# Last stage inside the experts' program, expert loops written out, first table loads spread, two evictions deferred

## The chip, the cores and the metric

The kernel runs on one core of a Trainium2 chip. The metric is the device time of one execution in microseconds. A core has five engines that run their own instruction streams and meet at semaphores: TensorE (PE, matmul, with its weight load PEld), VectorE (DVE), ScalarE (ACT), GpSimd (POOL) and SyncE (SP, which here only issues DMAs). Sixteen DMA engines move data between HBM and SBUF; SyncE, ScalarE and GpSimd issue to them.

## The reference, cut to what matters

Input x is 4096 tokens of 512 values. Two residual layers follow each other:

```python
x = x + layernorm(scan(layernorm(x)))      # selective scan, 512 channels x 16 states
x = x + layernorm(moe(layernorm(x)))       # 8 experts, top 2, capacity 640 per choice, plus a shared expert

# scan: xp = x @ W_x ; dt = softplus(xp[:64] @ W_dt + b_dt)
#       h = exp(dt * A) * h + (dt * x) * B ; y = sum(h * C) + x * D_skip
# moe, for each of the two choices k and each expert e (tokens beyond the capacity are dropped):
h = gelu(einsum('ecd,edf->ecf', buf, w1) + b1)                 # 512 -> 2048
y = einsum('ecf,efd->ecd', h, w2) + b2                         # 2048 -> 512
y = y + einsum('ecr,erd->ecd', gelu(einsum('ecd,edr->ecr', buf, wd)), wu)   # rank 32
out = out + tok * w                                            # weighted, back to the token's row
# shared expert for all tokens, times 0.2
```

## The kernel before

The program is a row of blocks with a barrier between them.

**prepare** (lines 57 to 324) works on eight chunks of 512 tokens. Per chunk: load x, normalise, transpose, project to xp, form dt with softplus, form dt * x. Results go to HBM as xT_d, bc_d (the rows of B and C), dt_d and dtx_d. The tiles xpT, dt and dx have two buffers each, xn and xnT three. SyncE's stream is one loop over rounds i (line 139): load x of chunk i+2, store xT of i-1, bc of i-2, dt and dtx of i-3, each behind the wait for its tile. In round 5 it also calls load_first_scans (line 127): eight loads of Bt and eight of Ct, each two rows of bc_d broadcast to 128 partitions, 512 KB, and five loads of 256 KB for the first passes of the scan. They fill tiles that live on into the next block.

**mix** (line 375) runs the scan, unit by unit over 8 chunks of 64 units, and fills TensorE's gaps with the shared expert for seven of the eight groups of 512 tokens. The sum is in acc_d, x after the first layer in x1_d.

**experts** (line 1020) does the shared expert for the last group, the routing, and then eight experts. An expert has three blocks of 2, 4 and 4 token tiles (EB, line 1006). A block is `run`, one per engine: 17 steps j, of which step 0 is the low-rank pair and the other 16 the hidden chunks. In a step TensorE makes the up product (L1684) of step j+1 into psH, then the down product of step j (L1723 for the low rank, L1727 for the others) into psY; ScalarE applies gelu (L1283, L1289); VectorE splits the result into a high and a low half (L1489 to L1497), since every product is taken as three matmuls of halves. After the last step VectorE takes the n tiles of psY out with weight and bias (L1514) into yst, and GpSimd adds them to acc_d with an indirect DMA (L1405). TensorE's first low-rank matmul of the next block waits until all of those n are out (L1716).

Weights of the next expert are loaded by SyncE piece by piece into a ring of four raw buffers (L1183), cast to the high half by ScalarE (L1242) during block 2 as soon as TensorE is done with the old chunk, and subtracted to the low half by GpSimd (L1361). Each body starts on ScalarE with a copy of the expert's biases (b1e, L1339). GpSimd's order within a body is `steady` (L1450): gathers of token rows (L1366) and of slot weights (L1390), scatters (L1405), the subtractions for the next expert. Its gathers for the next expert need the slot indices, which VectorE writes (L1602) after block 1.

On each engine the experts 0 to 6 are a hardware loop (`Fori`, L1348, L1469, L1661, L1789) and the expert 7 is written out behind it; SyncE's loop (L1224) loads the weights of experts 1 to 7. A matmul of 512 columns follows the other at 0.23 us.

**tail** (line 1794) is a block of its own: for 16 groups of 256 tokens load the sum y (L1817) and x1 (L1818), statistics (L1844, L1847), square root on ScalarE (L1831), reciprocal and product (L1851, L1853), normalise on ScalarE (L1834), add x1 (L1860), store from GpSimd (L1824).

Of the kernel before, what the change touches and what calls it, by code (L numbers as in the profile page):

```python
# [56 lines left out]
def prepare(nc, sem, const, early, x, A_log, D_skip, W_x, W_dt, b_dt, dt_d, dtx_d, bc_d, xT_d):  # L57
# [4 lines left out]
    with ExitStack() as ctx:  # L62
# [41 lines left out]
        def _(sp):  # L104
# [34 lines left out]
            for i in steps(2, 4):  # L139
# [8 lines left out]
                if i == 5:  # L148
                    load_first_scans()
# [867 lines left out]
WEIGH_AT = (4, 6, 8, 10)  # L1017


def experts(nc, sem, const, w, ws_d, lgT_d, x1_d, xt_d, acc_d, w_d):  # L1020
# [8 lines left out]
    with ExitStack() as ctx:  # L1029
# [3 lines left out]
        W1h, W1l = sb("W1h", [P, FC, DT, P], F32R), sb("W1l", [P, FC, DT, P], F32R)  # L1033
        W2h, W2l = sb("W2h", [P, FC, D], F32R), sb("W2l", [P, FC, D], F32R)
# [37 lines left out]
        Xa = (sb("Xah", [P, DT, 512], F32R), sb("Xal", [P, DT, 512], F32R))  # L1072
        X = (Xa, Xb, (sb("Xch", [P, DT, 256], F32R), sb("Xcl", [P, DT, 256], F32R)))
# [16 lines left out]
        s_spare, s_slots, s_sidx = (sem(f"c_{n}") for n in ("spare_rows", "slot_rows", "scatter_rows"))  # L1090
# [14 lines left out]
        g_sp, g_pool, g_pe, g_act, g_dve = (sem(f"c_gate_{n}") for n in ("sp", "pool", "pe", "act", "dve"))  # L1105
        block = ctx.enter_context(nc.Block("experts"))

# [6 lines left out]
        def shared(b):  # L1114

            return dict(B=0, t0=0, th=0, n=BT, gathered=False, row=b * BT)
# [46 lines left out]
        def added(e, i):  # L1163

            return (1 + e * Y_USES[i]) * 16

# [6 lines left out]
        def _(sp):  # L1173
# [50 lines left out]
            with sp.Fori(1, E) as e:  # L1224
                load_pieces(e + 1, weights_of(e))
                bias2(e, expert(e, 0))
            for i in range(4):
                sp.wait_ge(s_yst[i], added(E, i))
            for q in range(2):
                sp.wait_ge(s_xts[q], BT // 2 * 16)  # L1230

        @block.scalar
        def _(act):
# [27 lines left out]
            def weigh_bias(at, t):  # L1261

                if at["gathered"]:
# [5 lines left out]
                    scale = wsl[:, EB[k][0] + t:EB[k][0] + t + 1]  # L1269
                else:  # L1270
                    i, scale = t, SHARE
                    act.wait_ge(s_b2, 16)
                nc.scalar.mul(yst[i][:, :], b2bc[:, :], scale).then_inc(s_b2w, 1)
# [74 lines left out]
            with act.Fori(0, E - 1) as e:  # L1348
                expert_blocks(e)
            expert_blocks(E - 1, last=True)  # L1350

        @block.gpsimd
        def _(pool):
# [21 lines left out]
            def store_shared(b):  # L1375
                for t in range(BT):
                    pool.wait_ge(s_yev, t + 1)
                    nc.gpsimd.dma_start(acc_d[(b * BT + t) * P:(b * BT + t + 1) * P, :], yst[t][:, :])\
                        .then_inc(s_yst[t], 16)
# [30 lines left out]

            nc.gpsimd.memzero(L1h[:, :, :]).then_inc(s_pad, 1)
# [30 lines left out]
            store_shared(SB - 1)  # L1442
# [4 lines left out]
            gathers(0, 1, range(4))  # L1447
# [21 lines left out]
            with pool.Fori(0, E - 1) as e:  # L1469
                steady(e)  # L1470
            steady(E - 1, last=True)

        @block.vector
        def _(dve):
# [6 lines left out]
            def run(at, logits=False, nxt=None, extra=None):  # L1481
                G, n = at["B"] * J, at["n"]
                for j in range(J):
# [10 lines left out]
                    else:  # L1494
# [3 lines left out]
                            .then_inc(s_hlo, 1)  # L1498
                    if logits and j == 0:
# [8 lines left out]
                dve.wait_ge(s_mm2, G + J)  # L1508
                for t in range(n):
                    dve.wait_ge(s_b2w, at["t0"] + t + 1)  # L1510
                    i, scale = t, SHARE
                    if at["gathered"]:
                        i, scale = Y_TILE[at["k"]][t], wsl[:, EB[at["k"]][0] + t:EB[at["k"]][0] + t + 1]
# [428 lines left out]
```

## Time and profile before

| | us |
|---|---|
| median of 3 runs | 3615.76 (3614.01 to 3616.12) |
| the profiled execution, its own time | 3623.88 |
| its span, first to last instruction | 3622.1 |
| busy in the span: TensorE, VectorE | 3161.7, 1848.0 |
| busy in the span: GpSimd, ScalarE | 1724.7, 1426.5 |
| DMA moved, mean | 463.61 MB, 128 GB/s |

The profile comes from one execution, the times from others; durations are read from the first and the result is set against the second. The stages follow each other almost without overlap, so they are read one at a time: for each, which engine is busy nearly all of it, and where even that one stands still. The chain that ended last, as the page gives it, reaches back only to the barrier at 3552 us and speaks of the last stage alone.

### The profile page before, as it was taken

The page shows a single profiled execution, that of the slowest core. Times are in us where ns is not written, and L with a number is a line of the kernel's source. Part 1 is how long each engine was busy: PE and PEld are TensorE (multiplying, and loading weights), DVE is VectorE, ACT ScalarE, POOL GpSimd, SP SyncE. Part 2 cuts the span into 40 slices and gives each one's busy share as a digit, 9 for nine tenths or more (in the row PEclk, how much of TensorE's full clock was granted, in tenths as well). Part 3 has the DMA queues.
Part 4 walks back from the last instruction along what each step waited for, and adds up shares of the span by engine and source line. Part 5 has one row for each costly group of instructions (what it writes and reads, how often), then busy time and mean ns, then how long its engine had stood idle before and what let it go on. Part 6 is the DMA issues. An engine that isn't in the chain of part 4 may idle for free. (4 is left out here: it accounts for less than half of the span.)

```text
span 3622.1 us, 45551 instructions
## 1 busy us (share of the span) xinstructions
PE 3161.7 (87%) x15191; PEld 2578.5 (71%) x15191; DVE 1848.0 (51%) x2708; ACT 1426.5 (39%) x2529; POOL 1724.7 (48%) x1576
## 2 busy tenths in 40 slices
PE   6445698988989988789999999999999999999990
PEld 3233477777777776678888888788888887888880
DVE  6489889898898981462222232223222322232225
ACT  7445576766766763311221321322213213222113
POOL 1067787888879884431341532513415325134101
PEclk8655699999999999879999999999999999999995
DMA  7848696796976945921330421412304214123008
GB/s 235 229 149 218 188 256 189 215 242 197 248 206 197 267 148 167 267 68 21 70 77 12 99 56 33 108 21 64 81 14 99 56 33 108 21 64 79 12 12 290
DMA packets 276932, 463.61 MB, mean 128 GB/s; under 512 B 32065, under 2 KB 107729, under 8 KB 276706
## 3 DMA queue, kind: packets, MB, share of 16 engines
q1 hardware_dynamic: 206656, 266.21, 26.1%
q0 software_dynamic: 68288, 194.06, 20.8%
q8 instruction: 133, 2.18, 0.2%
q14 instruction: 93, 0.76, 0.1%
q10 hardware_dynamic: 1762, 0.40, 0.1%
HBM read 363.44 MB, written 97.14 MB: 127 GB/s over the span
## 5 line engine op out<-in xcount | busy, mean ns | idle before, releaser
L1495 DVE CAST hh<-h 128x512 fp32r<-128x512 f32 (+1 forms) x400 | 170.6, 426 | 1290.2 <-ACT h L1289 1245.0
L823 POOL TENSOR_TENSOR u<-dtxs,Bt 128x512 f32<-128x512 f32 x512 | 671.1, 1348 | 168.9 <-DVE b_psA L726 151.0
L1289 ACT ACTIVATE h<-c_psH,b1e 128x512 f32<-128x512 f32 (+1 forms) x384 | 236.8, 617 | 1254.4 <-PE c_psH L1684 1212.5
L726 DVE TENSOR_TENSOR_SCAN b_psA<-b_psA,carry,u 128x512 f32<-128x512 f32 x512 | 656.3, 1282 | 65.0 <-ACT b_psA L596 62.4
L1727 PE MATMUL c_psY<-W2h,hh 128*128 128x512 f32 x1344 | 536.3, 399 | 4.9 <-DVE hl L1497 4.6
L931 PE MATMUL b_psY<-ident,pr 128*128 128x128 f32 x2048 | 350.2, 310 | 207.9 <-DVE pr L733 190.2
L1727 PE MATMUL c_psY<-W2l,hh 128*128 128x512 f32 x1344 | 526.9, 392 | 0.0
L1727 PE MATMUL c_psY<-W2h,hl 128*128 128x512 f32 x1344 | 526.4, 392 | 0.0
L1366 POOL DMA_INDIRECT xrow<-xt_d,idx x80 | 90.6, 1132 | 882.4 <-PE c_psT L1675 479.8
L931 PEld LDWEIGHTS b_psY<-ident,pr 128*128 128x128 f32 x2048 | 269.4, 158 | 293.4 <-DVE pr L733 240.5
L733 DVE TENSOR_TENSOR pr<-b_psA,Ct 128x512 f32<-128x512 f32 x512 | 354.0, 691 | 19.2 <-DMA Ct<-bc_d 1.6
L596 ACT ACTIVATE b_psA<-dts,A_neg 128x512 f32<-128x512 f32 x512 | 354.3, 692 | 16.1
L966 PE MATMUL b_psH<-Xh,w 128*128 128x512 f32 x896 | 319.5, 418 | 8.1 <-DMA w<-ws_d 8.0
L1361 POOL TENSOR_TENSOR W1l<-raw,W1h 128x512 fp32r<-128x512 f32 x128 | 193.4, 1511 | 263.5 <-ACT W1h L1242 263.3
L1727 PEld LDWEIGHTS c_psY<-W2h,hh 128*128 128x128 f32 x1344 | 254.1, 189 | 60.1 <-DVE hl L1497 12.0
L985 PE MATMUL b_psS<-w,hhs 128*128 128x512 f32 x896 | 294.4, 410 | 0.0
L1727 PEld LDWEIGHTS c_psY<-W2h,hl 128*128 128x128 f32 x1344 | 253.9, 189 | 55.1
L1727 PEld LDWEIGHTS c_psY<-W2l,hh 128*128 128x128 f32 x1344 | 254.3, 189 | 47.6 <-issue 0.2
L1497 DVE TENSOR_TENSOR hl<-h,hh 128x512 fp32r<-128x512 f32 (+1 forms) x400 | 257.6, 644 | 13.7
L1684 PE MATMUL c_psH<-Xbh,W1h 128*128 128x512 f32 x576 | 224.4, 390 | 0.0
L1684 PE MATMUL c_psH<-Xbh,W1l 128*128 128x512 f32 x576 | 224.2, 389 | 0.0
L1684 PE MATMUL c_psH<-Xbl,W1h 128*128 128x512 f32 x576 | 224.1, 389 | 0.0
(262 smaller groups left out, 5763.0 us busy)
## 6 DMA issues: line engine op xcount, KB each, us to landing
w<-ws_d POOLq DMA_DIRECT2D x224, 512.0 KB, 6.8
raw<-in_w SPq DMA_DIRECT2D x256, 256.0 KB
Bt<-bc_d SPq DMA_DIRECT2D x64, 512.0 KB, 16.9
Ct<-bc_d SPq DMA_DIRECT2D x64, 512.0 KB, 20.5
xn<-in_x SPq DMA_DIRECT2D x8, 1024.0 KB, 6.3
xT_d<-xnT SPq DMA_DIRECT2D x8, 1024.0 KB, 8.5
dt_d<-a_dt SPq DMA_DIRECT2D x8, 1024.0 KB, 9.5
dtx_d<-a_dx SPq DMA_DIRECT2D x8, 1024.0 KB, 10.0
```

The costliest lines, as they stand in the source:

```text
L596: nc.scalar.activation(psA[g % 2][:, :], dts[s % 2][:, :], ACT.Exp, scale=A_neg[:, s % DT, n:n + 1]).then_inc(s_dA, 1)
L726: nc.vector.tensor_tensor_scan(psA[q][:, :], psA[q][:, :], u[g % U_RING][:, :], carry[:, k:k + 1], ALU.mult, ALU.add).then_inc(s_h, 1)
L733: nc.vector.tensor_tensor(pr[g % PR_RING][:, :], psA[g % 2][:, :], C_of(g), ALU.mult)\
L823: nc.gpsimd.tensor_tensor(u[g % U_RING][:, :], dtx[s % 2][:, :], Bt[n // TG][:, n % TG, :], ALU.mult)\
L931: last = nc.tensor.matmul(psY[:, t, :], pr[g % PR_RING][:, t * P:(t + 1) * P], ident[:, :], start=(n == 0 and t == 0), stop=False, is_tran ...
L966: last = nc.tensor.matmul(psH[:, :], a[:, d, :], v[:, d, :], start=(d == 0 and i == 0), stop=(d == DT - 1 and i == 2))
L985: last = nc.tensor.matmul(psS[t][:, :], a, v, start=False, stop=(j == FC and i == 2))
L1289: nc.scalar.activation(h32[:, 0:n * P], psH[j % 2][:, 0:n * P], ACT.Gelu, bias=b1[:, j - 1:j]).then_inc(s_gelu, 1)
L1361: nc.gpsimd.tensor_tensor(lo, view, hi.bitcast(F32), ALU.subtract).then_inc(s_wlo, 1)
L1497: nc.vector.tensor_tensor(hl[j % 2][a], h32[a], hh[j % 2][a].bitcast(F32), ALU.subtract)\
L1684: last = nc.tensor.matmul(out, a, b, start=(i == 0), stop=(i == n - 1))
L1727: last = nc.tensor.matmul(psY[t][:, :], a[j % 2][:, c], b, start=False, stop=(j == J - 1 and i == 2))
```

## The change

1. SyncE in prepare: load_first_scans is split. A pair of table loads (Bt and Ct of index i-3) follows the stores of each round from 3 to 10, and the loads of the first passes are made in round 9.
2. The four engines' loops over experts 0 to 6 and SyncE's over 1 to 7 become Python loops, so that eight bodies stand in a row.
3. In `run` on VectorE the last step takes out psY tiles 0 and 1 only. Tiles 2 and 3 of a block of four are taken out in the next block, after its step 0 (`late`). TensorE's low-rank matmuls of a gathered block wait for the eviction of their own tile. The shared block uses the same tiles and weight column as an expert's block 2, with the factor 0.2 set in the column at the start, and GpSimd stores it behind two gathers for expert 0.
4. The block `tail` is gone. Its instructions stand behind the experts on each engine, without a barrier. The x1 loads (L1818 before) are made during the last block of the last expert, paced by the up products; the loads of y when the last scatter has landed. Sixteen tiles each of y and x1 lie where x, W1 and W2 lay. SyncE waits for the final stores.

```diff
-            def load_first_scans():
+            def load_first_tables(j):
                 sp.wait_ge(s_obc[0], 16)
-                for j in range(NG):
-                    load_table(sp, bc_d, early["Bt"], early["s_B"], 0, j, 0)
-                    load_table(sp, bc_d, early["Ct"], early["s_C"], NS, j, 0)
+                load_table(sp, bc_d, early["Bt"], early["s_B"], 0, j, 0)
+                load_table(sp, bc_d, early["Ct"], early["s_C"], NS, j, 0)
+
+            def load_first_passes():
...
-                if i == 5:
-                    load_first_scans()
+                if 0 <= i - 3 < NG:
+                    load_first_tables(i - 3)
+                if i == NCH + 1:
+                    load_first_passes()
...
-            with sp.Fori(1, E) as e:
+            for e in range(1, E):
                 load_pieces(e + 1, weights_of(e))
                 bias2(e, expert(e, 0))
+            for g in range(NT // TAIL_G):
+                G = expert(E - 1, 2)["B"] * J
+                sp.wait_ge(s_mm1, G if g < 5 else G + min(J, 2 * g - 7))
+                sp.dma_start(x1r[g][:, :, :], tail_rows(x1_d, g)).then_inc(d_x1[g], 16)
+            sp.wait_ge(s_mm2, E * 3 * J + J)
             for i in range(4):
                 sp.wait_ge(s_yst[i], added(E, i))
+            for g in range(NT // TAIL_G):
+                sp.dma_start(y[g][:, :, :], tail_rows(acc_d, g)).then_inc(d_y[g], 16)
...
+            def leave(at, t):
+                dve.wait_ge(s_mm2, (at["B"] + 1) * J)
+                dve.wait_ge(s_b2w, at["t0"] + t + 1)
+                out, scale = y_out(at, t)
+                nc.vector.scalar_tensor_tensor(out, psY[t][:, :], scale, out, ALU.mult, ALU.add).then_inc(s_yev, 1)
...
+                    if late is not None and j == 0:
+                        for t in (2, 3):
+                            leave(late, t)
...
-                for t in range(n):
...
+                for t in range(2):
+                    leave(at, t)
...
-                run(expert(e, 0), nxt=(expert(e, 1), X_OF[1]), extra={12: (lambda: scatter_rows(e),)})
+                run(expert(e, 0), late=expert(e - 1, 2), nxt=(expert(e, 1), X_OF[1]), extra={12: (lambda: scatter_rows(e),)})
...
-                run(expert(e, 2), nxt=None if last else (expert(e + 1, 0), X_OF[0]))
-
-            with dve.Fori(0, E - 1) as e:
+                run(expert(e, 2), late=expert(e, 1), nxt=None if last else (expert(e + 1, 0), X_OF[0]))
+
+            for e in range(E - 1):
                 expert_blocks(e)
...
-                        after(pe, s_yev, at["t0"])
...
+                            if at["gathered"]:
+                                pe.wait_ge(s_yev, at["t0"] - (2 if at["k"] == 1 else 4) + min(t, 1 if at["k"] == 1 else 3) + 1)
```

## Rows read from the trace of the kernel before

**Rows 1.** Busy time by stage: stretch, length, each engine busy (instructions), clock, DMA share, GB/s.

```profile
0.00:198.00 198.00, 96.60 (x256) 47.99 (x256) 107.70 (x112) 110.31 (x113) 14.08 (x40) 0.72 0.75 223
198.00:1441.00 1243.00, 1038.83 (x5216) 841.26 (x5216) 1065.16 (x1219) 772.93 (x1459) 994.08 (x943) 0.88 0.74 208
1609.00:3536.00 1927.00, 1894.60 (x9132) 1579.44 (x9130) 539.34 (x1011) 467.59 (x827) 625.64 (x484) 0.99 0.24 54
3552.00:3622.10 70.10, 0.00 (x0) 0.00 (x0) 46.54 (x128) 28.68 (x49) 11.76 (x16) 0.50 0.94 359
```

**Rows 2.** The same view, three stretches inside the first stage (PE, PEld, DVE, ACT, POOL).

```profile
40.00:60.00 20.00, 14.95 (x36) 7.12 (x35) 14.87 (x15) 15.44 (x17) 1.66 (x4) 0.70 0.65 226
...
100.00:118.00 18.00, 12.95 (x33) 6.45 (x32) 10.40 (x5) 13.49 (x15) 0.24 (x2) 0.72 0.95 166
118.00:145.00 27.00, 0.20 (x2) 0.00 (x0) 3.52 (x2) 1.03 (x1) 0.00 (x0) 0.54 0.98 222
```

**Rows 3.** Timelines of ACT, then DVE: start, us, instruction, [idle before, releaser].

```profile
145.46 0.58 ACT L215 COPY xpT<-a_psX 96x512 f32<-96x512 f32 x1 [26.43 <-DMA bc_d<-xpT]
...
75.05 2.29 DVE L259 TENSOR_TENSOR a_dx<-a_dt,xnT 128x2048 f32<-128x2048 f32 x1
...
109.21 2.29 DVE L259 TENSOR_TENSOR a_dx<-a_dt,xnT 128x2048 f32<-128x2048 f32 x1
...
153.94 2.29 DVE L259 TENSOR_TENSOR a_dx<-a_dt,xnT 128x2048 f32<-128x2048 f32 x1
...
189.28 2.29 DVE L259 TENSOR_TENSOR a_dx<-a_dt,xnT 128x2048 f32<-128x2048 f32 x1
```

**Rows 4.** Timeline of SyncE's queue: first and last of sixteen table loads, next store.

```profile
77.77 1.05 SPq L330 DMA_DIRECT2D Bt<-bc_d  x1
...
113.13 3.19 SPq L330 DMA_DIRECT2D Ct<-bc_d  x1
...
127.20 5.57 SPq L119 DMA_DIRECT2D bc_d<-xpT  x1
```

**Rows 5.** TensorE by body, cut at each seam's last matmul: busy, clock, DMA share, GB/s.

```profile
3055.83:3298.60 242.77, 237.82 (x1144) 0.99 0.26 59
3298.60:3536.20 237.60, 235.36 (x1136) 0.99 0.13 23
sum 1688.71, PE 1657.86; mean PE 236.84
```

**Rows 6.** Second and seventh seam on PE, and ScalarE's wait (total, times, longest).

```profile
2090.62 0.36 PE L1684 MATMUL c_psH<-Xch,L1h 128*104 128x256 f32 x1 [0.76 <-POOL W1l L1361]
...
2097.06 1.22 PE L1723 MATMUL c_psY<-L,hh 96*128 96x512 f32 x2 [3.38 <-DVE hh L1492]
...
3303.94 0.70 PE L1723 MATMUL c_psY<-L,hh 96*128 96x512 f32 x2 [2.19 <-DVE hh L1492]
...
ACT b1e L1339 <- issue: 14.7, 6, 2.5
```

**Rows 7.** PE's waits over the experts: total us, times, longest.

```profile
PE c_psY L1727 <- DVE hl L1497: 4.4, 5, 1.3
```

**Rows 8.** Busy time right after the second seam (columns as in rows 1).

```profile
2096.00:2104.00 8.00, 6.94 (x26) 6.17 (x27) 2.77 (x7) 0.95 (x2) 6.78 (x5) 0.57 0.89 145
```

**Rows 9.** Timeline of DVE: the evictions of the shared block.

```profile
1570.02 2.48 DVE L1514 SCALAR_TENSOR_TENSOR yst<-c_psY,yst 128x512 f32<-128x512 f32 x4 [3.49 <-PE c_psY L1727]
```

**Rows 10.** From block 1 to block 2 of one expert, on DVE and PE.

```profile
2244.19 0.68 DVE L1492 TENSOR_TENSOR hh<-h,hl 32x512 fp32r<-32x512 f32 x1
...
2245.21 1.09 PE L1723 MATMUL c_psY<-L,hh 96*128 96x512 f32 x4
```

**Rows 11.** From the last scatter's landing to the load, then DVE's first and last statistics.

```profile
3549.20:3552.03 2.83, 0.00 (x0) 0.00 (x0) 0.00 (x0) 0.00 (x1) 0.00 (x0) 0.50 0.00 0
...
3555.86 1.29 DVE L1844 BATCH_NORM_STATS2 d_st<-d_y 128x6 f32<-128x512 f32 x2 [16.90 <-DMA d_y<-acc_d]
...
3609.94 1.28 DVE L1844 BATCH_NORM_STATS2 d_st<-d_y 128x6 f32<-128x512 f32 x2 [0.93 <-DMA d_y<-acc_d]
```

More of the change, by code:

```diff
@@ L1346, in expert_blocks @@
                     run(expert(e, 2), b1e, nxt=nxt(e + 1, 0), wset=e + 2)
-            with act.Fori(0, E - 1) as e:
+            for e in range(E - 1):
                 expert_blocks(e)
             expert_blocks(E - 1, last=True)
+            for g in range(NT // TAIL_G):
+                act.wait_ge(d_mv, (g + 1) * TAIL_G)
+                nc.scalar.activation(ours(sd, g), ours(mv, g)[:, :, 1], ACT.Sqrt, bias=eps[:, :]).then_inc(d_sd, 1)
+                act.wait_ge(d_nm, g + 1)
+                for t in range(TAIL_G):
+                    k = g * TAIL_G + t
+                    nc.scalar.activation(y[g][:, t, :], y[g][:, t, :], ACT.Identity, bias=nm[:, k:k + 1],
+                                         scale=rs[:, k:k + 1]).then_inc(d_n, 1)
         @block.gpsimd
@@ L1446, in _ @@
             gather_weights(0, 0)
-            gathers(0, 1, range(4))
+            gathers(0, 1, range(2))
+            store_shared(SB - 1)
+            gathers(0, 1, range(2, 4))
             gather_weights(0, 1)
@@ L1467, in steady @@
                     gather_weights(e + 1, 1)
-            with pool.Fori(0, E - 1) as e:
+            for e in range(E - 1):
                 steady(e)
             steady(E - 1, last=True)
+            for g in range(NT // TAIL_G):
+                pool.wait_ge(d_x, (g + 1) * TAIL_G)
+                nc.gpsimd.dma_start(tail_rows(out_d, g), y[g][:, :, :]).then_inc(d_out, 16)
         @block.vector
@@ L1658, in expert_blocks, with stats, scale, residual @@
                     expert_slots(e + 1)
-                run(expert(e, 2), nxt=None if last else (expert(e + 1, 0), X_OF[0]))
-            with dve.Fori(0, E - 1) as e:
+                run(expert(e, 2), late=expert(e, 1), nxt=None if last else (expert(e + 1, 0), X_OF[0]))
+            for e in range(E - 1):
                 expert_blocks(e)
             expert_blocks(E - 1, last=True)
+            for t in (2, 3):
+                leave(expert(E - 1, 2), t)
+            def stats(g):
+                dve.wait_ge(d_y[g], 16)
+                for t in range(TAIL_G):
+                    v.bn_stats(st[:, g * TAIL_G + t, :], y[g][:, t, :]).then_inc(d_st, 1)
+                for t in range(TAIL_G):
+                    dve.wait_ge(d_st, g * TAIL_G + t + 1)
+                    v.bn_aggr(mv[:, g * TAIL_G + t, :], st[:, g * TAIL_G + t, :]).then_inc(d_mv, 1)
+            def scale(g):
+                dve.wait_ge(d_sd, g + 1)
+                v.reciprocal(ours(rs, g), ours(sd, g)).then_inc(d_rs, 1)
+                dve.wait_ge(d_rs, g + 1)
+                v.scalar_tensor_tensor(ours(nm, g), ours(mv, g)[:, :, 0], -1.0, ours(rs, g), ALU.mult, ALU.mult)\
+                    .then_inc(d_nm, 1)
+            def residual(g):
+                dve.wait_ge(d_x1[g], 16)
+                for t in range(TAIL_G):
+                    dve.wait_ge(d_n, g * TAIL_G + t + 1)
+                    v.tensor_tensor(y[g][:, t, :], y[g][:, t, :], x1r[g][:, t, :], ALU.add).then_inc(d_x, 1)
+            for g in range(NT // TAIL_G + 2):
+                if g < NT // TAIL_G:
+                    stats(g)
+                if 1 <= g <= NT // TAIL_G:
+                    scale(g - 1)
+                if g >= 2:
+                    residual(g - 2)
         @block.tensor
@@ L1923, in program @@
         const["wgt"] = ctx.enter_context(nc.sbuf_tensor("wgt", [P, K, NT], F32))
[L1924 to L1925 removed]
+        experts(nc, sem, const, a, ws_d, lgT_d, x1_d, xt_d, acc_d, w_d, out)
 def kernel(**inputs):
```

124 lines of the change are left out of this document (36 added, 88 removed).

## The prediction

> **What bounds the kernel now.** I read the busy time by stage first, then what idles inside each stage, since no engine sets the end everywhere. [rows 1]: in the first stage (normalise, project, step sizes, 0 to 198 us) no engine is above 0.56 busy, but the DMA engines stand at 0.75. In the scan stage (198 to 1441) VectorE is busy 1065 of 1243 us. In the experts (1609 to 3536) TensorE is busy 1895 of 1927 us. In the last stage (3552 to the end) TensorE does nothing, VectorE is busy 46.5 of 70.1 us, and 359 GB/s move. The diff touches the first, third and last of these; the scan stage keeps its code and can only be moved as a block.
>
> The second view is where the first stage idles. [rows 2]: from 118 to 145 us TensorE works 0.2, VectorE 3.5 and ScalarE 1.0 us, while the DMA engines are at 0.98. [rows 3]: ScalarE waits 26.43 us there for one small store (bc_d) to land, so that the fourth and fifth L259 on VectorE stand 44.7 us apart, where two earlier gaps took 17.1 us each. [rows 4]: SyncE issued sixteen table loads (Bt, Ct) in one run from 77.77 to 116.3 us; the stores of the next chunk could only be issued behind them.
>
> The third view is the time per expert [rows 5], the fourth the seam between two experts [rows 6].
>
> **Part 1, table loads spread over the first stage.** Removed: the run of sixteen loads before the stores of chunk 3. Added: a pair after the stores of each of the eight chunks, and the five loads of the first passes two rounds before the end. Same bytes, same queue. The stall is 44.7 - 17.1 = 27.6 us. What is late next: a DMA queue without room. A chunk takes 17.1 us, in which the queue without tables is busy at 0.65 [rows 2], 11.1 us. During the run the tables move at 166 GB/s and 0.95 [rows 2], so a pair of 2 x 0.524 MB costs 6.3 x 0.95 = 6.0 us. Sum 17.1 us of 17.1: just full for three rounds, and looser after them, as no more x is loaded. A dt buffer is wanted again only two rounds after its store is due, so a lag of a few microseconds is covered; without that cover each microsecond of lag is one of the end. The last pair is queued behind the last stores and is first used some 34 us into the scan stage (unit 14, at 1243/512 = 2.4 us a unit). I take **-26 us**, between -10 (a full queue gives most back) and -28.
>
> Other edges of SyncE's queue: the waits of a round are unchanged, and the load of x for the next round now stands behind a pair of tables; it has a round and more to land.
>
> The Trainium skill, DMA: Bandwidth & Descriptors, in "Issuing engines are not separate DMA queues", says that all DMAs run on the same 16 engines and interleave, whoever starts them. By that rule moving loads creates no room, and only the idle 0.35 of the earlier rounds can be won. Rows 2 fit it, 0.65 and 0.95 being the two levels; by the rule alone the sum would still be up to -26, so it prices the first rival and changes nothing else.
>
> **Part 2, the bodies written out.** The row for the cost of a loop is the wait of ScalarE for nothing that the profile shows, ahead of the first copy of an expert: 14.7 us in six times, 2.5 us each [rows 6]. There are seven seams, and the seventh is the one from the loop to the body that is already written out. TensorE's first matmul after a seam waits 0.76 us where the loop jumps, and the low-rank matmul (L1723) 3.38 us, against 2.19 us at the seventh [rows 6]; from the last matmul of one expert (2089.47, 3298.60, the cuts of rows 5) to that one (2097.06, 3303.94) it is 7.6 us there and 5.3 us at the seventh. So the seventh seam shows what all will be: what remains is ScalarE's last weight casts and the chain gelu, three casts on VectorE.
>
> A better measure is the whole body. Six bodies take 1688.71 - 237.60 = 1451.1 us, 241.9 each; the last takes 237.60 [rows 5]. The last ends with its last matmul's end and not its start (0.4), and lacks the eight transposes for a next expert (1144 against 1136 matmuls; at the mean of 0.21 us per matmul they cost at most 1.7, being short I take 1.0). So a written-out body costs 237.6 - 0.4 + 1.0 = 238.2, which is 3.6 less, 6 x 3.6 = 21.9 us. That counts two things too much. The last body converts no weights, and a wait in midblock is absent from it: TensorE waits for VectorE's low half 4.4 us in five times [rows 7], when GpSimd's scatters stand ahead of the subtractions of weights. GpSimd starts that batch some 1.3 us earlier after the change, since the slot indices (L1602) follow two evictions and not four; I keep a third, 1.5 us.
>
> The clock: for 8 us after the seam the granted clock is 0.57 in a body that jumps [rows 8], which is mostly the lower level of 1.2 GHz, after the wait of 3.38 us. The last body has such a dip too (0.99 over it), so it is in the 238.2. If the shorter waits leave no dip, each full one is worth up to 8 x 0.43/0.5 = 6.9 us at half speed, 3.4 us; that is the far end of the gain.
>
> The Trainium skill, Runtime: NRT & Kernel Launch, "Instruction fetch mechanics", says that instructions are streamed ahead strictly in order and that a taken jump to code outside the window stalls its engine. The six waits of 2.5 us and their absence at the seventh seam agree.
>
> **Part 3, two of four evictions late.** VectorE now takes tiles 0 and 1 out of PSUM at once and tiles 2 and 3 after the low-rank casts of the next block, and TensorE waits per tile. For the shared block this frees VectorE two evictions earlier (2.48 us for four, so 1.2 us) [rows 9] on the chain into the slot search: **-1.2 us**, from 0 to -1.3. Within an expert it adds a wait: from block 1 to block 2 the cast chain ends at 2244.87 and TensorE starts the four low-rank matmuls at 2245.21, done in 1.09 us [rows 10]. The two late evictions (0.62 us each by rows 9, a little more from a full block) end near 2246.2, so the fourth matmul, due at 2245.9, waits some 0.3 to 0.4 us: 8 x 0.4 = 3.2 us lost. Behind it on TensorE's queue stands the next up product; the gelu that feeds VectorE waits on that. At the seams the next block has two tiles and meets no such wait. From 0 (the matmul still fits) to 10 us (each wait also holds VectorE's next cast). The store of the shared block's last two tiles moves behind two gathers on GpSimd, and bias products on ScalarE wait for it four steps later; covered.
>
> Parts 2 and 3 in the experts: -21.9 + 1.5 + 3.2 = **-17 us**, between -6 and -28.
>
> **Part 4, the last stage in the same program.** The x1 loads (8.4 MB) move under the last expert, whose DMA share is 0.13 [rows 5]: hidden, as 8.4 MB over its last block (0.4 of 237.6 us) are 88 GB/s; uncovered they would cost 8.4 MB at 359 GB/s, 23 us. The barrier goes: from the landing of the last scatter at 3549.20 to 3552.03 nothing moves [rows 11], -2.8. First data then takes 3.83 us as now. The last group's statistics start at 3609.94, 54.1 us after the first, 3.61 per group [rows 11], set by 25.2 MB at 359 GB/s. With 16.8 MB that would take 47 us to the last store, with 3.8 to the first data and the closing 12.2 us (3609.94 to the end) partly inside it, so VectorE takes over: 46.54 / 16 = 2.91 per group, 15 x 2.91 = 43.6. Gain 10.4 + 2.8 = **-13.2 us**. Ends: -9 (GpSimd's closing drain with sixteen stores behind it) and -15.
>
> **Sum.** -26 - 1.2 - 17 - 13.2 = -57.4 us. The profiled execution took 3623.88 us (span 3622.1, 1.8 outside it), 8.1 above the median of the shown runs; nothing in the terms scales with that, so I take the sum off the median: 3615.76 - 57.4 = **3558 us**.
>
> **Rivals.**
> (a) The queue is full: the pairs do not fit, the stores lag, and only 10 us come from part 1: 3558 + 16 = 3574. For it: 17.1 of 17.1. Against it: three rounds only, and slack of a round per buffer.
> (b) The loops give little: the late evictions and ScalarE's casts eat the seams, -6: 3558 + 11 = 3569. For it: the seventh seam still waits 2.19 us. Against it: the last body's 237.6.
> (c) The clock stays at its upper level over the shorter seams: 3.4 x 3 or more off: about 3548.
> (d) Slower: the written-out bodies cannot be fed. Eight bodies of code are then read in one go by every engine, and if an engine waits for code inside a body, TensorE waits with it. It decides once the price passes 57.4 / 7 = 8.2 us per body, over three waits of the 2.5 us that a jump costs now; at five it gives 3558 + 7 x 12.5 = 3646. Against it: the scan stage is written out already, and VectorE is busy 0.86 of it [rows 1].
> (e) It does not do what it says: the first-stage stall has another cause and the seams stay; -13 of part 4 only, 3603.
>
> **Chances.** Forecast (3549 to 3568) 0.62; (a) 0.12, (b) 0.11, (c) 0.09, (d) 0.03, (e) 0.03. The range reaches (a), (b) and (c) with their own spread: 3542 to 3581. A measurement of this kernel tells about 0.2%, 7 us, from no change. Faster 0.96, same 0.01, slower 0.03.
>
> **What would show it.** Part 1: L259 eight times at 17 to 18 us, the scan stage beginning near 172. Part 2: ScalarE's wait before L1339 gone, bodies of 238 to 239 us. Part 3: an idle of 0.3 to 0.5 us before one L1723 in each block 2. Part 4: loads of y right at the last landing, VectorE never idle in the end stage, some 57 to 59 us from landing to end. The largest risk is part 1: half of the sum rests on a queue that is full to its edge.

## The result, and the profile after

| | before | after |
|---|---|---|
| median of four executions (us) | 3615.48 | 3586.01 |
| lowest to highest (us) | 3614.01 to 3616.12 | 3580.53 to 3587.25 |
| profiled execution (us) | 3623.88 | 3580.53 |
| its span (us) | 3622.1 | 3578.8 |

The ratio is 0.9914, with a 95% interval of 0.9898 to 0.9930: **29.5 us less**, where 57 us less were forecast. The time lies above the range, which ended at 3581. The profiled execution of before lay 8 us above its median and that of after 5 us below its own, so the two traces differ by 43.3 us; of these, 14 belong to the two executions and not to the kernels.

Busy time by stage of the kernel after (columns as in rows 1, which these lines answer; the stages start earlier, so the cuts differ):

```profile
0.00:167.00 167.00, 94.74 (x256) 47.38 (x256) 107.71 (x112) 110.21 (x113) 14.09 (x40) 0.80 0.84 257
167.00:1411.00 1244.00, 1035.57 (x5216) 838.95 (x5216) 1065.61 (x1220) 775.14 (x1461) 996.13 (x959) 0.88 0.74 209
1580.34:3507.66 1927.32, 1910.80 (x9128) 1577.98 (x9128) 543.81 (x1011) 466.18 (x826) 632.64 (x487) 1.00 0.25 59
3507.66:3578.80 71.14, 0.03 (x1) 0.00 (x0) 48.38 (x132) 27.39 (x48) 17.97 (x20) 0.52 0.76 259
```

The first stage is some 31 us shorter at the same busy times. The experts' stage, from the first up product of the first expert to the last matmul, takes 1927.3 us where [rows 1] have 1927.0: no gain, but the inside has changed. TensorE is busy 1910.8 us of it and not 1894.6. **The waits went, and the same matmuls (some 9130) got longer.** That is the finding of this study.

The traces, stretch by stretch (each length from the first matmul of one part to the first of the next):

| stretch (us) | before | after | change | forecast |
|---|---|---|---|---|
| start to shared block | 1473.5 | 1441.5 | -31.9 | -26 |
| shared block | 137.6 | 138.8 | +1.2 | -1.2 |
| experts, first up product to last matmul | 1924.7 | 1926.9 | +2.2 | -17 |
| last matmul to end | 86.3 | 71.5 | -14.8 | -13.2 |

**First stage.** VectorE's timeline, the eight L262 (L259 before), answers [rows 3]; first three, fifth to last:

```profile
40.76 2.29 DVE L262 TENSOR_TENSOR a_dx<-a_dt,xnT 128x2048 f32<-128x2048 f32 x1
57.93 2.29 DVE L262 TENSOR_TENSOR a_dx<-a_dt,xnT 128x2048 f32<-128x2048 f32 x1
75.05 2.29 DVE L262 TENSOR_TENSOR a_dx<-a_dt,xnT 128x2048 f32<-128x2048 f32 x1
...
109.22 2.29 DVE L262 TENSOR_TENSOR a_dx<-a_dt,xnT 128x2048 f32<-128x2048 f32 x1
126.29 2.29 DVE L262 TENSOR_TENSOR a_dx<-a_dt,xnT 128x2048 f32<-128x2048 f32 x1
143.36 2.29 DVE L262 TENSOR_TENSOR a_dx<-a_dt,xnT 128x2048 f32<-128x2048 f32 x1
160.20 2.29 DVE L262 TENSOR_TENSOR a_dx<-a_dt,xnT 128x2048 f32<-128x2048 f32 x1
```

They stand 17.1 us apart from the first to the last; the gap of 44.7 us is gone. The stretches that answer [rows 2] show where the tables now move:

```profile
40.00:60.00 20.00, 14.95 (x36) 7.07 (x35) 15.95 (x15) 15.72 (x17) 1.66 (x4) 0.76 0.98 274
...
100.00:118.00 18.00, 12.05 (x33) 6.04 (x32) 10.44 (x6) 14.62 (x16) 0.00 (x0) 0.81 0.83 267
118.00:145.00 27.00, 15.00 (x29) 6.92 (x30) 20.09 (x10) 14.45 (x13) 0.00 (x0) 0.75 0.76 210
```

From 40 to 60 us the DMA engines go from 0.65 to 0.98, full as the sum had it, and no engine loses time by it.

**Waits in the experts.** The waits of TensorE over the experts, all that the view gives, answer [rows 6, 7] (engine, line waited at, releaser: total, times, longest; L1809 is the low-rank matmul, L1723 before):

```profile
PE c_psY L1809 <- DVE hh L1549: 8.5, 4, 2.6
PE c_psY L1809 <- issue: 6.4, 3, 2.5
PE c_psH L1769 <- DVE Xcl L1529: 1.5, 1, 1.5
PE c_psY L1809 <- DVE yst L1536: 1.3, 8, 0.2
```

The seven seams wait 8.5 + 6.4 us in all, 2.1 each, as the seventh of before did. The wait for hl in midblock is gone, and so is ScalarE's wait ahead of the first copy. New is the wait for the late evictions in each of eight experts; on the timeline of TensorE and VectorE in one of them:

```profile
1731.42 1.41 DVE L1536 SCALAR_TENSOR_TENSOR yst<-c_psY,slot_weights,yst 128x512 f32<-128x512 f32 x2
...
1731.71 1.01 PE L1809 MATMUL c_psY<-L,hh 96*128 96x512 f32 x3
1732.88 0.50 PE L1809 MATMUL c_psY<-L,hh 96*128 96x512 f32 x1 [0.16 <-DVE yst L1536]
```

The fourth low-rank matmul starts 0.66 us after the third, where 0.23 is usual (all four of before follow each other at 0.23 to 0.24). The third comes 0.28 us after the second and the next up product 0.34 us after the fourth, so that the late evictions cost 0.59 us here; the view counts only the 0.16 us in which nothing at all ran.

**Tail.** SyncE's load, then VectorE's first and last statistics (these answer [rows 11]):

```profile
3520.41 17.84 SPq L1264 DMA_DIRECT2D d_y<-acc_d  x16
3524.28 1.29 DVE L1724 BATCH_NORM_STATS2 d_st<-d_y 128x6 f32<-128x512 f32 x2 [13.82 <-DMA d_y<-acc_d]
...
3565.12 1.28 DVE L1724 BATCH_NORM_STATS2 d_st<-d_y 128x6 f32<-128x512 f32 x2
```

From the landing of the last scatter to the end it is 58.4 us. VectorE's sixteen groups stand 2.72 us apart on the mean instead of 3.61: the first two last only 1.42 and 1.63 us, as no x1 is added yet, and from the fourth on it is 2.87 us. From 3524.28 to 3567.30 VectorE is busy 42.14 us of 43.02.

**Where the gain of the experts went.** The groups of TensorE's matmuls by form, over 1620 to 3450 us, of the kernel before (count, then total busy us and mean ns of one):

```profile
L1727 PE MATMUL c_psY<-W2l,hh 128*128 128x512 f32 x1214 | 476.3, 392 | 0.0
...
L1684 PE MATMUL c_psH<-Xah,W1l 128*128 128x512 f32 x512 | 201.8, 394 | 0.0
L1684 PE MATMUL c_psH<-Xah,W1h 128*128 128x512 f32 x512 | 201.8, 394 | 0.0
...
L1684 PE MATMUL c_psH<-Xbh,W1h 128*128 128x512 f32 x451 | 175.7, 389 | 0.0
```

and of the kernel after:

```profile
L1813 PE MATMUL c_psY<-W2l,hh 128*128 128x512 f32 x1214 | 480.6, 396 | 0.0
L1813 PE MATMUL c_psY<-W2h,hl 128*128 128x512 f32 x1214 | 480.2, 396 | 0.0
L1769 PE MATMUL c_psH<-Xah,W1l 128*128 128x512 f32 x512 | 200.6, 392 | 0.0
...
L1769 PE MATMUL c_psH<-Xbh,W1h 128*128 128x512 f32 x474 | 187.4, 395 | 0.0
```

Already before, the same product on the same shape took 394 ns from Xa and 389 from Xb. After, Xb and the down products are at 395 and 396. The ends are modelled, so the better measure is the spacing of starts between matmuls of one kind (mean of all under 0.3 us): before 0.2269 us for Xb, 0.2333 for Xa and 0.2281 for the down products; after 0.2319, 0.2293 and 0.2335. What the diff changed for them is only the order in which the tiles are declared, and with it their addresses: W1 and W2 stood ahead of all other tiles of the experts and now stand behind Xa and Xc (the lines that do it, others left out):

```diff
-        W1h, W1l = sb("W1h", [P, FC, DT, P], F32R), sb("W1l", [P, FC, DT, P], F32R)
-        W2h, W2l = sb("W2h", [P, FC, D], F32R), sb("W2l", [P, FC, D], F32R)
...
         rt.close()
...
+        X = (Xa, Xb, (sb("Xch", [P, DT, 256], F32R, loop), sb("Xcl", [P, DT, 256], F32R, loop)))
+        W1h, W1l = (sb(f"W1{h}", [P, FC, DT, P], F32R, loop) for h in "hl")
+        W2h, W2l = (sb(f"W2{h}", [P, FC, D], F32R, loop) for h in "hl")
```

### The profile page after: what moved, and what is told of

It reads as the page before. It is cut to its first block, busy times and chain, and to the rows that moved or that the text cites. A ratio compares the mean times of both kernels' runs of the same rounds, so it can differ in the third digit from the quotient of the medians.

```text
span 3578.8 us, 43069 instructions
## 1 busy us (share of the span) xinstructions
PE 3174.4 (89%) x15191; PEld 2574.6 (72%) x15191; DVE 1854.1 (52%) x2708; ACT 1425.5 (40%) x2529; POOL 1732.0 (48%) x1577
## 4 chain that ended last, share of the span: by engine, by line
PE 55%; DVE 2%; DMA 1%; issue 1%; POOL 1%; ACT 1%; SPq 0%; POOLq 0%; DVEq 0%; ACTq 0%
PE c_psH L1769 27%; PE c_psY L1813 26%; PE c_psT L1760 1%; PE c_psT L1864 1%; DVE d_y L1740 1%; DVE d_st L1724 1%; PE c_psY L1809 0%; DVE yst L1536 0%; DMA xrow<-x_d 0%; DMA raw<-in_w 0%; POOL W1l L1406 0%; DVE hh L1546 0%; ACT h L1320 0%; POOL W2l L1406 0%; DMA acc_d<-yst,sidx 0%
## 5 line engine op out<-in xcount | busy, mean ns | idle before, releaser
L599 ACT ACTIVATE b_psA<-dts,A_neg 128x512 f32<-128x512 f32 x512 | 354.3, 692 | 16.1
L1451 POOL DMA_INDIRECT acc_d<-yst,sidx x80 | 130.4, 1629 | 203.3 <-DVE yst L1536 182.3
```

The lines of the kernel that those rows point to most:

```text
L599: nc.scalar.activation(psA[g % 2][:, :], dts[s % 2][:, :], ACT.Exp, scale=A_neg[:, s % DT, n:n + 1]).then_inc(s_dA, 1)
```

## The experiments

The tables give start addresses in SBUF modulo 256 bytes, counted from the sizes in the order of declaration. A **pad** is an unused tile that does nothing but move what is declared behind it. Of a matmul's two operands the stationary one is what PEld loads (W1 in an up product, a slice of hh or hl in a down product), and the moving one is X or W2. Theory P: the place of the two operands against each other sets the spacing. Its rivals: the written-out code is fed more slowly (P's pad would then change nothing), or another engine's traffic on SBUF slows the reads.

**The pad in the kernel after.** W1, W2, Xa and Xc move by 64 bytes:

```
         loop = ExitStack()
+        sb("pad", [P, 16], F32, loop)
         Xa = (sb("Xah", ...
```

> The changed kernel with 64 unused bytes per partition ahead of the tiles Xa, Xc, W1 and W2, which moves these to start at 32 modulo 128 bytes, as Xb, hh and hl do. Nothing else differs. Theory P (placement): a matmul of 512 columns follows the other at 0.227 us where its moving and its stationary operand start at the same place modulo 128, and at 0.232 to 0.234 us where they don't; in the changed kernel that slows every down product and the up products of block 2. Then the last block of four tiles takes 90.6 + 0.6 us instead of 93.3, a body about 4.4 us less, and the whole kernel 30 to 36 us less than the changed kernel: ratio to before 0.982 to 0.984, about 3553 us. Rival D (distance): what counts is how far apart the operands lie, which 64 bytes don't change; then it equals the changed kernel, ratio 0.991. Rival S (the stream of written-out code slows TensorE's issue): also no change.

Measured: 3555.54 us (3554.92 to 3558.40), ratio 0.9824 [0.9811, 0.9838]. Block 1, block 2 and the last block of the last expert, first of the kernel after, then of the padded one (here only PE, clock, DMA share and GB/s in the first fence; all engines in the second):

```profile
1631.88:1726.10 94.22, 94.22 (x417) 1.00 0.07 12
1726.10:1820.56 94.46, 94.30 (x409) 1.00 0.40 103
...
3413.95:3507.66 93.71, 93.55 (x401) 1.00 0.29 80
```

```profile
1634.86:1727.58 92.72, 92.72 (x418) 76.43 (x417) 23.27 (x41) 15.95 (x25) 10.62 (x8) 1.00 0.07 12
1727.58:1819.99 92.41, 92.25 (x410) 75.58 (x409) 28.28 (x42) 31.76 (x57) 54.59 (x41) 1.00 0.42 105
...
3393.05:3484.64 91.59, 91.44 (x402) 74.66 (x400) 22.16 (x39) 15.34 (x22) 6.54 (x4) 1.00 0.30 81
```

TensorE is busy without a gap in block 1 in both, with the same matmuls at the same clock, and takes 1.50 us less with the pad; in block 2 it is 2.05 us less. The experts take 1900.5 us instead of 1926.9. Nothing but addresses differs: placement sets the spacing, and the code feed is ruled out as its cause. Which tiles' places count is the question of the next runs.

**The pad in the kernel before**, ahead of Xa alone:

```
+        sb("pad", [P, 16])
         Xa = (sb("Xah", ...
```

> The kernel before with 64 unused bytes per partition ahead of Xa and Xc, so that these too start at 32 modulo 128 bytes like W1. Theory P: block 1 of each expert (up products with Xa, 192 matmuls) and block 0 (Xc) get faster, 192 x 6 ns = 1.2 us and some 0.2 us per body, 10 to 12 us in all: ratio 0.997, block 1 at 93.0 instead of 94.2 us. Rivals D and S: no change, ratio 1.000.

Measured: 3613.40 us, ratio 0.9980 [0.9970, 0.9989] of the kernel before. Block 1 takes 92.72 us instead of 94.2, in eight bodies 11.6 us less; the experts 1916.6 instead of 1924.7, since the waits in midblock were longer in this execution (block 2 in seven bodies 657.4 us against 654.0). The group of Xa's products is now equal to Xb's:

```profile
L1685 PE MATMUL c_psH<-Xah,W1h 128*128 128x512 f32 x512 | 199.4, 389 | 0.0
...
L1685 PE MATMUL c_psH<-Xbh,W1h 128*128 128x512 f32 x456 | 177.6, 389 | 0.0
```

**What distance counts.** Three more places in the kernel before, by pads of 128 and 32 bytes behind W1 and W2, and of 64 bytes ahead of them (block 1 and time in us):

> The kernel before with 128 bytes of unused SBUF behind the expert weights, so that all activations move by 128 bytes against W1 and W2 and keep their place modulo 128. If the place modulo 128 bytes decides: matmuls keep their spacings, 0.2268 us for the up products from Xb and all down products and 0.2335 for those from Xa, block 1 at 94.2 us, and the time stays at the kernel before's, about 3617. If it is modulo 256 or more: the products that were at 0.2268 go to 0.2335, 480 x 0.0067 = 3.2 us more per expert, 26 us in all, about 3643.

> The kernel before with 64 bytes of unused SBUF ahead of everything of the experts, so that weights and activations move together. Modulo 256 bytes, W1, W2, Xb and hh then stand at 224 (160 before) and Xa at 160 (96 before): every distance is as before. Theory D (the distance between the two operands decides): spacings stay at 0.2269 for the up products from Xb and 0.2333 for those from Xa, time near 3618. Rival A (the place itself decides, 160 being a good one): the products from Xb and the down products lose up to 0.0064 us each, block 1 goes from 94.2 to near 95 us, and the time is up to 26 us longer, 3640.

> The kernel before with 32 bytes of unused SBUF behind the expert weights: modulo 256 W1 and W2 at 160, Xb and hh at 192, Xa at 128. Theory D (only equal places are fast): products from Xb and the down products, now 32 bytes apart, go from 0.2269 to about 0.233, Xa's (now 32 apart the other way) stay slow; time near 3643, as with 128 bytes (3639). Rival H (places within the same 64 bytes are as good as equal): Xa's products at 128 stand in the 64 bytes of W1's 160 and get fast, Xb's and the down products at 192 get slow; 480 down and 176 up products slower, 176 faster, by 0.0064 us in eight bodies: about 24 us longer.

| kernel | W1, W2 | Xb, hh | Xa | spacing Xb | spacing Xa | down | block 1 | time |
|---|---|---|---|---|---|---|---|---|
| before | 160 | 160 | 96 | 0.2269 | 0.2333 | 0.2281 | 94.2 | 3615.5 |
| before, all + 64 | 224 | 224 | 160 | 0.2270 | 0.2333 | 0.2283 | 94.2 | 3615.8 |
| before, pad at Xa | 160 | 160 | 160 | 0.2270 | 0.2270 | 0.2281 | 92.7 | 3613.4 |
| before, + 128 | 160 | 32 | 224 | 0.2331 | 0.2302 | 0.2331 | 94.4 | 3639.4 |
| before, + 32 | 160 | 192 | 128 | 0.2333 | 0.2334 | 0.2329 | 94.9 | 3656.4 |
| after | 96 | 160 | 96 | 0.2319 | 0.2293 | 0.2335 | 94.2 | 3586.0 |
| after, pad at Xa | 160 | 160 | 160 | 0.2270 | 0.2270 | 0.2280 | 92.7 | 3555.5 |

My rule of modulo 128, under which the first pad was made, falls: 128 bytes of distance cost as much as 64 or 32. Moving both operands together changes nothing, so it is the distance that counts and not the place. The rival that another engine's traffic decides falls for Xb: with 32 or 128 bytes more, Xb keeps its distance from h32, hh and hl, which other engines write, and of the matmuls' tiles only W1 and W2 stand elsewhere; its products get slow all the same. Every fast pair stands at distance 0 modulo 256; 512 is not needed, as W1 and Xb of before differ by 256 there (17568 and 154016). All pairs at another distance are slow, by 1.4 to 2.9%, and the sign seems to matter: with the moving operand 64 bytes above the stationary one it is 0.2302 and 0.2319, with it 64 bytes below 0.2333 to 0.2335. One pair fits only in part: Xa and W1 of the kernel after are at distance 0 and still have 0.2293. There hh, hl and h32 stand 64 bytes off, while every fast pair comes from a kernel in which W1, W2, hh and the X in use all stand at one place; no run moves hh alone, so it is not shown that a pair's own distance is all that counts. The times of the three shifted kernels are single executions. That of 3656.4 is 13 us longer than spacings explain: 6.6 us of it stand ahead of the shared block (which starts at 1476.1, against 1469.5 in the kernel with all + 64), where the code is the same.

**The tables alone** (the first part of the change, nothing else):

```
-                if i == 5:
-                    load_first_scans()
+                if 0 <= i - 3 < NG:
+                    load_first_tables(i - 3)
+                if i == NCH + 1:
+                    load_first_passes()
```

> The kernel before with only the table loads of the first stage spread over the rounds (part 1 of the change). My forecast was -26 us; the changed kernel's trace has the scan stage's end 31 us earlier. If part 1 alone does that and the rest of the loss is in the experts: -26 to -32 us, 3584 to 3589, ratio 0.991 to 0.993. If part of it is given back later by another stage: less. Everything after the scan stage as in the kernel before.

Measured: 3593.63 us, ratio 0.9926 [0.9911, 0.9942], **26.7 us less**; the experts' shared block starts at 1441.2 us. The kernel before, run once more beside it, took 3618.50 us and started that block at 1469.9:

> The kernel before itself, for a second profile. Its profiled execution took 8 us more than its median, the changed kernel's 5 us less. If the 8 us are the short spells of TensorE at the lower clock behind the seams, they are in this profile at other seams or fewer, and the span is 3613 to 3622 us. Stage ends otherwise within 1 us of the first profile.

So 28.7 us between these two traces. That the first pair of traces showed 31.9 is the profiled execution of before, late by 3.6 us there; part of its 8 us above the median. Over all sixteen traces of this study the shared block starts at 1467.6 to 1476.4 us in the six without the spread tables and at 1440.6 to 1446.4 in the ten with them; the means differ by 28.7.

**The loops alone**, put back into the padded kernel on all five engines:

```
-            for e in range(E - 1):
+            with pe.Fori(0, E - 1) as e:
```

> The padded kernel after with the loops over the experts back on all five engines; tables, evictions, last stage and addresses as in the padded one (3555.5 us). Theory J (the jump costs at the seam only): TensorE's first low-rank matmul of an expert comes 7.6 - 5.3 = 2.3 us later at each of six seams, and the one entry into the loop costs about as much again, 14 to 16 us, plus up to three lower-clock stretches of 3.4 us: 3570 to 3581, ScalarE's waits for nothing of 2.5 us back ahead of the first copy, and no wait in the middle of block 2, since that went with the later evictions. Rival B (the loop costs what the last body of the kernel before suggested, 3.6 us each): 6 x 3.6 = 22 us, 3577. Rival M (the wait in midblock came with the loop, GpSimd's jump putting its scatters ahead of the subtractions): that wait of 4.4 us is back in several bodies, and 3580 to 3595. Rival N: the loops cost nothing that matters, under 3 us, 3558.

Measured: 3572.92 us (3563.93 to 3574.13), ratio 0.9871 [0.9853, 0.9889] against 0.9824 without loops: 17 us by the ratios, 11.5 us by the experts' stage of the traces (1912.0 against 1900.5), whose execution is the fastest of its four. ScalarE's waits and TensorE's at the seams are back:

```profile
ACT b1e L1377 <- issue: 14.3, 6, 2.6
...
PE c_psY L1810 <- DVE hh L1550: 11.8, 4, 3.3
PE c_psY L1810 <- issue: 9.2, 3, 3.1
```

21.0 us at seven seams instead of 14.9 to 16.0, and 0.6 to 1.1 us more before TensorE's first matmul behind each jump. The wait in midblock is not back, so rival M falls: the loop did not make it. Rival N falls too. Between theory J and rival B the time does not decide, as the two intervals leave some 8 us on either side of the 17; the stage of the traces, 11.5 us, speaks for J. The Trainium skill, Runtime: NRT & Kernel Launch, "Instruction fetch mechanics", says that a taken jump out of what has been read ahead stalls its engine, while the cost of code in a row is mostly hidden: these rows agree, the wait being there six times for six jumps and at no seam of the written-out form.

**The late evictions.** All four at once again, in the padded kernel, TensorE waiting for the last:

```
-                    if late is not None and j == 0:
-                        for t in (2, 3):
-                            leave(late, t)
...
-                for t in range(2):
+                for t in range(n):
                     leave(at, t)
```

> The padded kernel after with all four evictions at once and TensorE waiting for the last of them; loops written out, tables and last stage as changed. Theory L (the late evictions cost 0.6 us in each of eight experts at the change to block 2, and win little elsewhere): about 5 us faster in the blocks 2, 1.2 us slower in the shared block, and at the seams 2 x 0.62 us slower seven times, since the next low-rank matmuls now stand behind four evictions: sum -5 + 1.2 + 8.7 = 5 us slower, 3560. Rival M (the slot indices, and so GpSimd's batch, start 1.3 us later, and the wait of 4.4 us in midblock comes back in most bodies): 3560 + 5 to 8 times 4.4 us, 3582 to 3595. Rival F (seams are bound elsewhere, by the weight casts): 3551, faster than the padded one.

and late only at the seams, block 1's four at once with the slot indices after the second:

```
-                run(expert(e, 1), nxt=(expert(e, 2), X_OF[2]))
-                if not last:
-                    expert_slots(e + 1)
-                run(expert(e, 2), late=expert(e, 1), nxt=None if last else (expert(e + 1, 0), X_OF[0]))
+                run(expert(e, 1), nxt=(expert(e, 2), X_OF[2]), rest=lambda: None if last else expert_slots(e + 1))
+                run(expert(e, 2), nxt=None if last else (expert(e + 1, 0), X_OF[0]))
```

(`run` calls `rest` behind its first two evictions and then makes the other two.)

> The padded kernel after, but inside an expert the four evictions of block 1 stand at once (slot indices after the first two), and only the two at a seam stay late. Theory L: the wait of 0.6 us before a low-rank matmul in block 2 goes in eight experts, -4.8 us, 3550.7; block 2 at 91.8 us instead of 92.4. Rival: TensorE's low-rank matmuls now stand behind four evictions and lose the same 0.6 us elsewhere, no change, 3555. Other side: the evictions delay the casts that the low-rank matmuls wait for by 1.2 us each, +9.6 - 4.8 = 5 us slower, 3560.

The first gave 3560.41 us (ratio 0.9839 [0.9820, 0.9859]), the second 3552.45 (0.9819 [0.9798, 0.9841]), on another chip than the padded kernel and with intervals that overlap. So all three forms ran once more side by side on one chip:

> The padded kernel after once more (evictions 3 and 4 late everywhere), as the base for the two forms beside it on the same chip: ratio to the kernel before 0.982 as in its first run (3555.5 us of 3620.3).

> Late evictions only at the seams between experts. If the traces' 3.9 us in the experts are real, the median lies 3 to 5 us under that of the padded kernel in the same call; if they were the scatter of the lower-clock stretches, within 1.5 us of it.

> All four evictions at once. If the wait in the middle of block 2 (0.5 to 2.5 us in seven experts in its first trace, 9.5 us in all) outweighs the 0.6 us of the late form (4.8 us in all), the median lies 3 to 6 us over that of the padded kernel in the same call; if the two cancel, within 1.5 us of it.

| form | median (us) | ratio | experts, trace (us) |
|---|---|---|---|
| two late everywhere | 3554.62 | 0.9823 [0.9804, 0.9842] | 1899.8 |
| late at seams only | 3556.36 | 0.9827 [0.9807, 0.9846] | 1899.2 |
| all at once | 3559.78 | 0.9839 [0.9820, 0.9859] | 1905.9 |

TensorE's waits in the third form:

```profile
PE c_psY L1805 <- DVE hh L1550: 15.3, 7, 2.5
PE c_psY L1809 <- DVE hl L1555: 7.1, 6, 1.6
```

and in the second:

```profile
PE c_psY L1812 <- DVE hh L1550: 16.5, 7, 3.2
PE c_psY L1816 <- DVE hl L1555: 1.5, 4, 0.6
```

The wait for hl in midblock, 25.8 us into block 2, belongs to the order of VectorE's queue: it is there when the slot indices stand behind all four evictions (7.1 us here, 6.6 in the first run of this form), small when they stand behind two with the other two next, and absent when they stand behind two alone. The late evictions as a whole seem to win about 5 us (3559.78 against 3554.62, and the same 5 us in the pair before), but the intervals overlap in both pairs; the experts' stages of the traces say 6.1, and 2.6 in the pair before. The second form wins nothing: my 4 us of its first run were scatter. It trades the 0.6 us of the late matmul (block 2 at 91.8 us at best instead of 92.4) for midblock waits, in four bodies of this trace and one of the first. At the seams all three forms wait alike, 15 to 17 us in seven: what ends last there is the cast of hh on VectorE, and not the evictions.

**The earlier x1 loads**, undone in the padded kernel:

```
-            for g in range(NT // TAIL_G):
...
-                sp.dma_start(x1r[g][:, :, :], tail_rows(x1_d, g)).then_inc(d_x1[g], 16)
...
             for g in range(NT // TAIL_G):
                 sp.dma_start(y[g][:, :, :], tail_rows(acc_d, g)).then_inc(d_y[g], 16)
+                sp.dma_start(x1r[g][:, :, :], tail_rows(x1_d, g)).then_inc(d_x1[g], 16)
```

> The padded kernel after with the sixteen loads of x1 issued after the last scatter, one behind each load of y, as the kernel before had them; the end stage stays in the experts' program, without the barrier. Theory (the 10.4 us that the prediction gave to the earlier loads are real): the end stage is bound again by 25.2 MB at about 359 GB/s, and the time rises by 10.4 us, from 3555.5 to 3566. Rival: the end stage is bound by VectorE's order and the chain through ScalarE in both forms, and the gain is the barrier's; under 3 us, 3555 to 3558.

Measured: 3568.43 us, ratio 0.9858 [0.9841, 0.9874], **12.9 us more** than the padded kernel (12.3 by the ratios, as the two ran on different chips). VectorE's first and last statistics of this kernel:

```profile
3499.25 1.29 DVE L1721 BATCH_NORM_STATS2 d_st<-d_y 128x6 f32<-128x512 f32 x2 [13.71 <-DMA d_y<-acc_d]
...
3553.71 1.29 DVE L1721 BATCH_NORM_STATS2 d_st<-d_y 128x6 f32<-128x512 f32 x2 [0.93 <-DMA d_y<-acc_d]
```

They are 54.5 us apart, as in [rows 11], and 40.8 in the kernel after: the end stage is bound by the DMA engines with these loads in it and by VectorE without them.

## Why the prediction was off

**Part 1, -26: right.** Alone it gave -26.7. The queue was full in the early rounds and held, so rival (a) falls; L262 came in the promised step, and the scan stage started 31 us earlier in the first pair of traces. The Trainium skill, DMA: Bandwidth & Descriptors, "Issuing engines are not separate DMA queues", says that all DMAs run on the same 16 engines, whoever starts them. The trace fits it: what was won is idle time of those engines, whose share rose to 0.98 in the rounds where it had been 0.65.

**Part 3 in the shared block, -1.2: no gain shows.** With Xb and W1 at one place it takes 136.8 to 138.2 us in the six traces with two late evictions and 136.9 to 137.9 in the seven with four at once: what two evictions less ahead of the slot search bring is lost in the scatter. In the kernel after it is 138.8, by the spacings of its up and down products; the kernels with 32 and 128 bytes have 138.9 and 139.3.

**Parts 2 and 3 in the experts, -17: right in the sum once the operands are back in place, in part by luck.** With the operands of both kernels at distance 0, the experts' stage goes from 1916.6 (before with its pad) to 1900.5 and 1899.8 (after with its pad): -16.1 and -16.8. (These are single traces; in four traces of before's loops and operands the stage takes 1921.5 to 1927.0 us.) The terms were off in opposite directions. The loops bring 11.5 us by traces and up to 17 by ratios, where -21.9 + 1.5 = -20.4 stood, most of it for them. The late wait costs 8 x 0.64 = 5.1 us in the padded kernel instead of 3.2, but the midblock wait is gone entirely and not kept to a third, so that the late evictions, priced as a loss of 3.2, seem to be a gain of about 5. Rival (b) falls. Rival (c) can't be told from scatter: stretches at the lower clock behind the seams sum to 34.0 us in the trace of before and 13.6 in that of after, but to 17.0 to 34.0 in the eight traces with loops and 13.6 to 23.8 in the eight without. The means, 27.6 and 17.0, are 5 us of work apart at half speed.

**The step that failed** is the sentence "So the seventh seam shows what all will be", used for whole bodies. It took 237.60 us of the last body as the price of the same matmuls in the new kernel. The diff moved four tiles (the halves of W1 and W2) behind others, and I gave that nothing. The bodies of the kernel after take 240.3 to 242.0 us from last matmul to last matmul; with the pad they take 236.8 to 238.7. Between the two padded kernels and the two as they are, the move costs 26.4 - 8.1 = 18.3 us in the experts' stage by traces, and -16.1 + 18.3 = +2.2 is what the traces show. By ratios, after loses 32 us against its padded form and before 7 us, 25 in all, and 3558 + 25 = 3583 is near the 3586 measured. Seen the other way, the two padded kernels differ by 0.9980 - 0.9824, which is 56 us, where 57.4 were forecast. The row was to be had before: 394 ns beside 389 ns for one product on one shape, the only difference being which tile it reads.

**Part 4, -13.2: right in the sum.** -14.8 by the traces. Its two terms were off in opposite directions: 12.9 us come from the loads where 10.4 stood, and the barrier's share is 1.3 to 2 us where 2.8 stood (86.3 us from the last matmul to the end before, 85.0 with the late loads and no barrier). The 10.4 priced every group at the mean of 2.91, 43.6 us for fifteen; they took 40.8, the first two being shorter. The 57 to 59 us from landing to end were 58.4.

**Rivals (d) and (e)** did not come. No engine waited for code inside a body for long enough to show in TensorE's waits, though (d) would have been believed from the body times alone: 240.3 to 242.0 us with written-out code, where 238 to 239 were promised. The pad was needed to tell them apart.

The padded kernel beats both: 3555.5 and, measured again, 3554.6 us, ratio 0.9823 [0.9804, 0.9842]. The 3558 of the forecast less the 7 us that before's own Xa lost would be 3551.

## What to carry to other kernels

When a diff reorders declarations, write the start addresses of both operands of the costly matmuls beside each other, before and after, and give the difference a term of its own; and when one product on one shape has two durations in the groups by form, find out why before the rows are used. Work that loads ahead of a DMA-bound end stage is worth its bytes at that stage's rate until the next engine binds (12.9 us for 8.4 MB here). A body measured at the end of a loop prices the others only for what the change leaves alone: its waits, and not its matmuls once tiles move.

## What the runs showed of the hardware that I had not expected

- Matmuls of 128x512 (fp32r), back to back at the upper clock, stood 0.2269 to 0.2283 us apart when the moving and the stationary operand started at the same place modulo 256 bytes of a partition, and 0.2302 to 0.2335 at distances of 32, 64 and 128 bytes. In the kernel after that makes 26.4 us of 1926.9 over the eight experts. Why is open: no run tells a conflict in reading the two operands from another one, and the 0.2293 at distance 0 in the kernel after, where hh and hl stand elsewhere, is not explained.
- A loop's jump cost 12 to 17 us for six jumps of five engines, about 2 to 3 us each. In the trace TensorE's low-rank matmul comes 1.8 us later at such a seam, 0.8 of it before its first matmul and the rest as later casts.
- Stretches of 3.4 us (a few of 6.8) at the lower clock came behind four to seven of the seven seams in the written-out forms, though TensorE stood still there for only 2.0 to 2.7 us (twice for 3.2 and 3.4). They differed from trace to trace, 13.6 to 23.8 us in all, which is up to 5 us of time. The start of the shared block scatters as much, 1440.6 to 1446.4 us with the same code up to it.
